# Attention batches of a fused transformer layer with a changed instruction order and other PSUM banks

## The reference, cut to what matters

```
h = concat(patches @ W + b, txt)                      # (8, 548, 192)
x = layernorm(h)
q, k, v = x@Wq.T, x@Wk.T, x@Wv.T                      # three heads of 64
scores = (q . k) / 8 * decay                          # decay = gamma**(m-l) for m >= l, else 0
weights = softmax(scores)                             # entries under the diagonal have score 0, not -inf
o = weights @ v
y = (o - mean) / sqrt(var + eps) * gn_weight + gn_bias   # mean and var per sequence and head
h = h + y @ Wo.T
x2 = layernorm(h)
probs = softmax(x2 @ router_w.T);  comb = the top 8 of 16, normalised to sum 1
h = h + sum over experts e of comb[e] * (gelu(x2 @ w1[e]) @ w2[e])
```

## Time and profile before

| | us |
|---|---|
| median of 3 runs | 796.58 (795.94 to 799.67) |
| the profiled execution, whole | 794.4 |
| its span, first to last instruction | 792.1 |
| mean granted TensorE clock | 0.981 of full |

### The profile page before, as it was taken

The page is one execution under the profiler, slowest core; times in us unless marked ns, Lnnn a source line. Parts: engine busy times, 40 slices in busy tenths (PEclk is TensorE's granted clock), DMA queues, the critical chain, the costliest instruction groups (busy, mean ns, idle before and its releaser), DMA issues.

```text
span 792.1 us, 13238 instructions
## 1 busy us (share of the span) xinstructions
PE 744.4 (94%) x4400; PEld 635.0 (80%) x4400; DVE 551.0 (70%) x1548; ACT 485.9 (61%) x1087; POOL 155.8 (20%) x261
## 2 busy tenths in 40 slices
PE   6688898999988999999999999999999999999997
PEld 2577787888886777788888888888888888888885
DVE  5588888889788676576567566576666666665654
ACT  1368897897886846456556456556465564564443
POOL 2034436535542780010010010010000100100000
PEclk9689999999998999999999999999999999999999
DMA  7500010011031462242242241342241332412410
GB/s 223 167 2 21 21 42 22 23 42 43 2 100 41 121 184 60 77 127 72 58 115 69 77 128 39 86 125 55 78 120 52 86 104 62 109 62 70 113 50 19
DMA packets 44390, 60.74 MB, mean 77 GB/s; under 512 B 4018, under 2 KB 37762, under 8 KB 44322
## 3 DMA queue, kind: packets, MB, share of 16 engines
q1 hardware_dynamic: 44322, 59.91, 26.5%
HBM read 51.84 MB, written 8.05 MB: 76 GB/s over the span
## 4 chain that ended last, share of the span: by engine, by line
PE 71%; ACT 12%; DVE 7%; issue 4%; POOL 3%; DVEq 1%; POOLq 1%; DMA 0%; SPq 0%
PE ps L1271 67%; ACT pt L595 3%; ACT pr L674 3%; DVE sc L982 2%; ACT ot L595 2%; ACT pr L642 1%; ACT k_hi L595 1%; DVE pr L1006 1%; PE ps L1400 1%; POOL w_lo L553 1%; PE ps L1451 1%; DVE nm L989 1%; ACT xa_hi L595 1%; DVE k_lo L945 1%; POOLq L552 1%
## 5 line engine op out<-in xcount | busy, mean ns | idle before, releaser
L1177 DVE TENSOR_TENSOR act<-act,gate 128x480 f32<-128x480 f32 (+1 forms) x216 | 144.8, 671 | 115.8 <-ACT act L788 110.7
L1271 PE MATMUL ps<-x,w_hi 128*128 128x480 f32 (+1 forms) x648 | 217.0, 389 | 0.2 <-ACT act L788 0.2
L788 ACT ACTIVATE act<-ps 128x480 f32<-128x480 f32 (+1 forms) x216 | 123.7, 573 | 130.2 <-PE ps L1271 130.1
L1271 PE MATMUL ps<-x,w_lo 128*128 128x480 f32 (+1 forms) x432 | 165.9, 384 | 0.0
L945 DVE TENSOR_TENSOR act_lo<-act,act_hi 128x480 fp32r<-128x480 f32 (+1 forms) x216 | 145.0, 671 | 0.2
L1271 PEld LDWEIGHTS ps<-x,w_hi 128*128 128x128 f32 x648 | 121.6, 188 | 21.2 <-ACT act L788 0.7
L595 ACT ACTIVATE act_hi<-act 128x480 fp32r<-128x480 f32 (+1 forms) x216 | 130.7, 605 | 6.8 <-DVE act L1177 6.7
L1271 PEld LDWEIGHTS ps<-x,w_lo 128*128 128x128 f32 x432 | 81.2, 188 | 13.4
L1271 PE MATMUL ps<-act_hi,w_hi 128*128 128x480 f32 (+1 forms) x216 | 83.5, 387 | 4.5 <-DVE act_lo L945 4.5
L1271 PE MATMUL ps<-act_hi,w_lo 128*128 128x480 f32 (+1 forms) x216 | 82.5, 382 | 0.0
L1271 PE MATMUL ps<-act_lo,w_hi 128*128 128x480 f32 (+1 forms) x216 | 82.5, 382 | 0.0
(11 more groups left out here) (181 smaller groups left out, 1257.0 us busy)
## 6 DMA issues: line engine op xcount, KB each, us to landing
gate<-comb_dram SPq DMA_DIRECT2D x112, 240.0 KB, 3.2
gate<-comb_dram SPq DMA_DIRECT2D x32, 256.0 KB, 3.8
w_raw<-w SPq DMA_DIRECT2D x16, 384.0 KB, 3.7
h_dram<-h SPq DMA_DIRECT2D x8, 384.0 KB
res<-h_dram SPq DMA_DIRECT2D x7, 360.0 KB, 4.4
out<-res SPq DMA_DIRECT2D x7, 360.0 KB, 3.2
h<-txt SPq DMA_DIRECT2D x3, 672.0 KB
decay_rows<-drow SPq DMA_DIRECT2D x1, 1014.0 KB, 8.4
```

The costliest lines, as they stand in the source:

```text
L788: a.activation(act[j % 3][:, 0:n], ps[:, up_bank(j), 0:n], ACT.Gelu_apprx_tanh).then_inc(gelu_done, 1)
L1177: dve.tensor_tensor(act[j % 3][:, 0:n], act[j % 3][:, 0:n], gate[e % 4][:, 0:n], ALU.mult).then_inc(gated, 1)
L1271: return pe.matmul(dst, w, x, start=start, stop=stop)
```

## The change

What it does, part by part:

1. Head 2's probabilities are scaled on VectorE alone, all five tiles; `scale_probs` and its semaphores go.
2. `qk` computes its tiles in the order 0, 1, 2, and both `qk_round` and `qk_rest` take k of heads 0 and 1 ahead of q and k of head 2. `scores_pair` then waits for the first two rests alone, and for the others ahead of row tile 2.
3. Head 2's o is copied once, to partitions 0 to 63, and no longer also to 64 to 127 (`Y_ROWS`). The copy of head 1's o moves from the end of the body into the next one, between the roundings of k and of head 2's q.
4. All banks are laid out anew, with the waits that go with them.
5. VectorE's order: `norm_stats(b+2)` moves from ahead of the decays to behind `add_attention`, and the first of `add_attention`'s three parts from ahead of `normalise(b, 1)` to behind it. GpSimd's: `halve_w1(b)` comes ahead of `rstd_of(b+2)`, and `y_values` has two more drains.
6. The last batch: batch 5 is projected and added in the middle of the body, like the others, and no longer at its end; the store of its h is issued in the body. The router's second transpose and its logits come later, `up(0)` and `up(1)` come around `comb_transpose`, and the four groups of head 2's transposes all stand ahead of `down(0)`. On ScalarE `exps(b, 2)` comes ahead of `comb_copy`.

The diff, cut to its core:

```diff
-X_BANKS = (6, 1)
-QK_BANKS = (4, 6, 1)
-SCORE_BANKS = [(2, 4), (0, 5), (2, 6)]
...
+X_BANKS = (1, 6)
+QK_BANKS = (4, 1, 6)
+SCORE_BANKS = [(0, 7), (3, 2), (0, 6)]
...
+Y_ROWS = (P, HD)
...                                   # GpSimd, body
+                halve_w1(b)
                 if ahead:
                     pool.drain()
                     rstd_of(b + 2, ln1_var, rstd, mv, veps, nmr, ln1_rstd)
-                halve_w1(b)
...                                   # ScalarE, body
                 qk_round(b, 0)
                 qk_round(b, 1)
                 if tail:
-                    scale_probs(t)
-                for part in (2, 3):
-                    qk_round(b, part)
+                    o_copy(t, 1, O_BANKS[1])
+                qk_round(b, 2)
+                qk_round(b, 3)
...
+                    x2_round(0, 0, LAST_X2[0])
+                    exps(b, 2, (0,))
+                    x2_round(0, 1, LAST_X2[1])
+                    pt_copy(b, 1)
+                    o_copy(b, 0, LAST_O[0])
+                    logits_exp(0)
+                    exps(b, 2, (1, 2, 3, 4))
+                    comb_copy(0, LAST_X2[1])
+                    o_copy(b, 1, LAST_O[1])
...                                   # VectorE, normalise and body
-                for I in range(2 if hh == 2 else 0, NT):
+                for I in range(NT):
...
-                if tail and ahead:
-                    dve.wait_ge(ln1_rstd, nth(b, 1, 2))
-                    norm_stats(b + 2, st6, mv, veps, ln1_var)
...
                 normalise(b, 0)
                 apply_decay(b, 2)
-                if later and more:
-                    add_attention(b - 2, WO_BANKS, (0,))
+                normalise(b, 1)
+                if later:
+                    add_attention(b - 2, WO_BANKS)
+                if ahead:
+                    dve.wait_ge(ln1_rstd, nth(b, 1, 2))
+                    norm_stats(b + 2, st6, mv, veps, ln1_var)
                 if not more:
-                    x2_rest(0, 0, 5)
-                    x2_rest(0, 1, 4)
-                normalise(b, 1)
-                if later and more:
-                    add_attention(b - 2, WO_BANKS, (1, 2))
...
+                    x2_rest(0, 0, LAST_X2[0])
+                    x2_rest(0, 1, LAST_X2[1])
...                                   # TensorE, scores_pair and body
-                pe.wait_ge(qk_lo, nth(b, 4, 4))
+                pe.wait_ge(qk_lo, nth(b, 4, 2))
                 if tail:
+                    pe.wait_ge(o_copied, nth(b - 1, 3, 2))
                     pe.wait_ge(pt_copied, nth(b - 1, 4 * H, 2 * 4 + 2))
...
-                    probs_transpose(t, 2, (0,))
-                    pe.wait_ge(o_copied, nth(t, 3, 2))
                     pe.wait_ge(qk_lo, nth(b, 4, 1))
-                    probs_transpose(t, 2, (1, 2, 3))
+                    probs_transpose(t, 2, (0, 1, 2))
+                    pe.wait_ge(qk_lo, nth(b, 4, 2))
+                    probs_transpose(t, 2, (3,))
...
                 if not more:
-                    logits(0, 4)
-                elif later:
-                    pe.wait_ge(wo_added, nth(b - 2, 3, 1))
+                    pe.wait_ge(pt_copied, nth(b, 4 * H, 2))
+                    x2_transpose(0, 0, LAST_X2[0])
                 attend(b, 0, O_BANKS[0])
+                if not more:
+                    pe.wait_ge(wo_added, nth(b - 2, 3, 3))
+                    x2_transpose(0, 1, LAST_X2[1])
                 probs_transpose(b, 1, (0, 1))
...
+                if not more:
+                    up(0)
+                    comb_transpose(0, LAST_X2[1])
+                    up(1)
...                                   # SyncE
-                if later and more:
+                if later:
                     store_h(b - 2)
...
             load_w2(3)
-            store_h(LB - 2)
             gates(0, 4, 5)
```

232 lines of the change are left out of this document (104 added, 128 removed).

## The result

The changed kernel took 800.47 us (median of 20 runs, 797.67 to 802.86), the kernel before 795.88 beside it (20 runs, 794.62 to 799.67). The ratio is 1.0053, with a 95% interval from 1.0042 to 1.0063: slower by half a per cent. The forecast was 800.6. The profiled execution took 801.78, its span is 799.0, 6.9 more than before. The median gap is 4.6 us, so the profiled pair shows about 2 us more than the typical pair. Both ends add to that: 801.78 is 1.3 above its median, and the profiled execution before, 794.4, is faster than all 20 runs beside it. So what follows from one profile against the other is an upper end, and the prices rest on the medians where there are any.

The account below looks back on a forecast made before the run. VectorE's own list was taken to set the pace in batches 1 to 5. Terms 4.0 - 0.9 + 0.1 + 0.8 = +4.0 us on the median of 796.58 gave 800.6, with an 8 in 10 range from 793.5 to 805.

Parts of the forecast that it names:

- Batches 2 to 5, +4.0 forecast: x_ext to x_ext in batches 2 to 5: period 29.25 against 28.22 us, +1.0 four times; bounds 0 to +6.4.
- D: VectorE's first decay in batches 2 to 5: 11.3 us behind x_ext instead of 12.30, after some 1.1 us of waiting.
- the 1.0: Each of batches 2 to 5: first decay 1.0 us earlier, but norm_stats adds 2.15 behind it; net +1.0 us.
- Batch 6, -0.9: Batch 6, with norm_stats in neither version: 27.1 against 28.02 us, since the earlier first decay is real there.
- Batches 0 and 1, +0.1: First two batches: gain up to 1.5 us from k's rest, mostly taken back by halve_w1; bounds -1.5 to +1.5.
- Scaling on VectorE, +0.78 per batch ahead of q: Head 2's scaling: five tiles take 1.58 us where three took 0.80, so VectorE has 0.78 more to do.
- The last batch, +0.8 forecast: Last batch and first expert tiles: gates 1.4 later, clock fall 3.0, less 3.6 given back; bounds -3.0 to +3.5.
- the 3.0: Last batch: TensorE's low clock goes from the logits but falls at the first experts instead, costing 3.0 us again.
- the 3.6: Experts' stage: most of VectorE's 2.36 us gate wait and TensorE's 3.18 us idle time given back, -3.6 us.
- The hole: Rival: VectorE's wait ahead of the first decay near nothing, clock holds; +0.8, 797.4; chance 0.27 with the no-effect rival.
- The last batch did not give through: Rival: TensorE's lead at up(1) reaches the end, weights' copy under 36 us behind last x_ext; -3.8, 792.8; chance 0.19.
- The shared port: Rival: GpSimd's y_values catches head 2's last scaling tile, batches 2 to 7 each 0.8 us longer; 805.4; chance 0.12.

Follow-up runs that it names:

- experiment 1: Changed kernel with norm_stats in batches 1 to 5 put back ahead of the first decay: 796.54 us against 796.63 for the kernel before, ratio 1.0001.
- experiment 3: Changed kernel plus nine unused matmuls in batches 1 to 6, filling TensorE's wait ahead of the q and k matmuls: 798.71 us, ratio 1.0022.
- experiment 2: Kernel before with only norm_stats moved behind the attention sums, ahead of gn_partial: 797.56 us against 796.63, ratio 1.0011.
- experiment 8: Kernel before with all five tiles of head 2 scaled on VectorE, none on ScalarE, in all batches: 800.18 us, ratio 1.0041.
- experiment 6: Changed kernel with norm_stats early again and two of head 2's five tiles scaled on ScalarE again: 798.79 us, ratio 1.0030.
- experiment 10: Changed kernel plus unused matmuls in the last batch, 16 behind up(1) and 20 behind head 2's first two transpose groups: 799.64 us, ratio 1.0027.
- experiment 9: Kernel before with head 2's first two tiles scaled on VectorE in the last batch alone: 800.61 us, ratio 1.0040.
- experiment 5: Changed kernel with norm_stats early again and the last batch's whole old order on all engines, with new banks: 797.05 us, ratio 1.0009.
- experiment 11: Changed kernel with norm_stats early, the last batch's old order, and two head 2 tiles scaled on ScalarE in the last batch alone: 794.55 us against 796.73, ratio 0.9970.
- experiment 7: Changed kernel with norm_stats early, two head 2 tiles scaled on ScalarE again, and the last batch's old order: 797.61 us, ratio 1.0015.

## Why the prediction was right, and where its sum was not

The direction and the size were right (+4.0 forecast, +4.6 in the medians), and so was the main mechanism: undoing the move of norm_stats takes the loss away (experiment 1). That 800.6 meets 800.47 so closely is luck. The forecast started from a median of three runs, 796.58, and the 20 runs have 795.88; and the terms, +4.0, -0.9, +0.1 and +0.8, were in the profile +4.85, +0.23, -0.85 and +2.67, together 6.9. The low clock in q and k, by the profiles half of what the move cost, was not in the sum at all.

*Batches 2 to 5, +4.0 forecast, +4.85 in the profile.* D at 11.3 was 11.24, the wait ahead of it 1.1 was 1.20, D to x_ext 17.97 was 17.61, the period 29.25 was 28.85 in batch 3. That is +0.63 for this batch, not +1.0. The prediction took batch 3 for all four, while before they ran from 27.78 to 28.69. Four times 28.85 against the 112.78 of before make 2.6; 1.46 more is batch 4's fall, which I did not have, and 0.75 more is batch 2 (29.60), of which below. I had named the wait at the start of q and k (1.00 + 0.28 us) and costed it at nothing, as idle time of an engine that waits for VectorE; experiment 3 shows that its price is the clock behind it. Two falls in this profile make 2.9 us. How many come differs by execution, which fits the spread from 797.67 to 802.86 and the mean clocks beside these times; where they lay was seen only in profiled executions.

*The working of the 1.0.* The prediction took norm_stats as free where it stood and as 2.15 where it went, and set against it a D that is 1.0 earlier. Against experiment 1 the late place costs 0.6 us in batches 3 to 5 (28.85 against 28.27). Had it stayed, the batch would be 28.3, not the 27.1 one might read from batch 6, since the new order leaves a hole of 1.2 us for 2.6 us of rows and gaps (9.95 to 12.56 behind x_ext). On the kernel before, the same move gave +0.9 us in the medians, not told from nothing, and 0.6 us a batch in the profile (experiment 2): TensorE's waits for ScalarE left D only 0.5 us earlier there. The edits that the prediction priced at nothing (head 2's o copied once, k rounded ahead, head 1's o copied later, the GpSimd order) and the new banks were not undone one by one; with all of them in place batches 3 to 5 of experiment 1 take 28.28, about what batch 3 took before.

*Batch 6, -0.9.* Measured +0.23, with a fall of 1.44 in it; without one 26.8 in seven kernels with the new layout and the scaling on VectorE, so -1.2. Right in kind.

*Batches 0 and 1, +0.1.* From x_ext to x_ext batch 0 took 0.02 and batch 1 0.14 more than before. The -0.85 comes from batch 0's x_ext, which was 1.01 earlier, and nothing here tells that from scatter.

*Scaling on VectorE, +0.78 per batch ahead of q.* It took 0.80 more (1.60 against the earlier trace rows), and costs nothing over the batches: in the old order VectorE waits for k's rounding anyway (experiment 8), and in the new order the alternative is worse by 1.6 in batch 6 (experiment 6).

*The last batch, +0.8 forecast, +2.67 measured.* This is the term that was mis-sized. Its pieces: gates 1.4 later (measured 1.3, the copy at 37.2, but by two errors that cancel: the logits began 4.5 us later, not 3.2, and from their start to the copy 7.1 us passed instead of 10.4, which is 3.3 less and not 1.8); the clock at 1.00 from logits to attend, and a fall at the experts behind a wait for copies of 3 to 4 us (measured 3.22), all as written. But the fall lasted 3.4 us, not the 6 of before that the 3.0 was worked out from, and costs 1.1 (experiment 10), and the 3.6 that later idle times were to give back did not come: in the 40 us window of the experts TensorE is busy for 36.48, before 36.82. And I had not asked what the scaling on VectorE does in the last batch, where no hole covers it: moved alone it lengthens the wait ahead of `down(0)` from 1.37 to 3.30 and costs 3.8 us in the profile, 3.2 by the ratio (experiment 9); with the old order on the new layout, experiments 5 and 11 differ by 3.1 us for it. The new order seems to have a cause of its own beside it, since with the scaling back on ScalarE the stretch is 569.32 in the new order and 566.18 in the old (experiments 6 and 7). This rests on one profile each, and experiment 11, nearly the same there as 7, had 568.66. How the 2.67 divide between the two is left open.

*The rivals.* The hole did not close (1.20 us of wait). The last batch did not give through: the copy came at 37.2, past the deciding 36. The shared port did not catch head 2's scaling in batch 3, where five tiles took 1.60 though GpSimd's tensor_scalar starts inside them (119.36). In batch 2 the rows read as the rival was written: the last tile is caught. VectorE there, the second row being the last of the five tiles by itself, and GpSimd there; then the last tile and GpSimd in batch 3:

```profile
88.90 2.06 DVE L996 TENSOR_SCALAR pr<-pr,inv_den 128x580 f32<-128x580 f32 x5
90.23 0.73 DVE L996 TENSOR_SCALAR pr<-pr,inv_den 36x68 f32<-36x68 f32 x1
```
```profile
89.73 1.19 POOL L527 TENSOR_SCALAR ot<-ot,gscale,gshift 128x548 f32<-128x548 f32 x1 [0.26 <-issue]
```
```profile
119.48 0.27 DVE L996 TENSOR_SCALAR pr<-pr,inv_den 36x68 f32<-36x68 f32 x1
```
```profile
119.36 0.90 POOL L527 TENSOR_SCALAR ot<-ot,gscale,gshift 128x548 f32<-128x548 f32 x1 [0.28 <-issue]
...
133.09 1.97 POOL L500 TENSOR_TENSOR w_lo<-w_raw,w_hi 128x384 fp32r<-128x384 f32 x2
```

In batch 2 GpSimd's instruction takes 1.19 instead of 0.90, and VectorE's last and smallest tile, which starts inside it, 0.73 instead of 0.27; that tile ends at 90.96, GpSimd's instruction at 90.92. So the scaling is 0.46 longer. VectorE is 0.81 late at q's rest (7.16 behind x_ext against 6.35), and the other 0.35 is a wait of 0.43 ahead of the reciprocal, before GpSimd's instruction starts, which no row explains. The batch is 0.75 longer than batch 3. No experiment separated this, so the port is read from the ends of the rows, for 0.46 us in one batch and not 0.8 in six. The old meeting is still there: VectorE's nm (134.07 + 1.02 = 135.09) ends with w_lo (135.06). Both meetings agree with the exclusive lock that the Trainium skill, "SBUF — State Buffer", section "SBUF: two separate sides", describes.

## What to carry to other kernels

A hole in an engine's list is worth something only together with the order that makes it: after each edit, ask anew what fits into it. Price a wait of TensorE twice, as idle time and as the chance of a slow clock in the matmuls behind it; filling the wait with matmuls that nobody reads is a quick test of which of the two you pay. And take a repeated edit apart by place: the same 0.8 us of scaling was useful in the batches of the new order, cost nothing in those of the old one, and cost 3 to 4 us in the last batch. Last, read the granted clock of every timed run before you trust a pair of profiles: here the profile before was one of that kernel's best executions.
